# Routed experts: ten single-expert tiles and eight tiles of four 32-token units, copied matrices in homes of their own, rotary step ahead of the FFN norm

## What is computed

```python
x = x + layernorm(attention(layernorm(x)))   # 16 heads of 16; low-rank q and kv; rotary part added to q and k
x = x + layernorm(ffn(layernorm(x)))
# ffn, 2048 tokens, 8 experts, top 1:
logits = x @ router_w.T ; e = argmax ; score = sigmoid(top logit)
gate, up = split((x * score) @ gate_up_proj[e])   # 256 -> 2 x 512
routed   = (up * silu(gate)) @ down_proj[e]       # 512 -> 256
shared   = silu(x @ shared_gate_w) * (x @ shared_up_w) @ shared_down_w
```

## Time and profile before

| | us |
|---|---|
| median of three executions | 446.71 |
| lowest, highest | 446.14, 450.4 |
| the profiled execution, whole | 448.61 |
| its span (first to last instruction in the trace) | 446.8 |
| PE busy in it | 414.9 |
| DVE busy | 254.1 |
| ACT busy | 197.4 |
| POOL busy | 133.4 |

### The profile page before, as it was taken

One profiled execution on the slowest core, in us unless ns is written; L12 is line 12 of the kernel. 1 busy time (PEld: TensorE's weight loads), 2 busy tenths in 40 slices (PEclk: granted clock), 3 DMA queues, 4 the chain that ended last, 5 costly groups with the idle time before them and its releaser, 6 DMA issues.

```text
span 446.8 us, 8888 instructions
## 1 busy us (share of the span) xinstructions
PE 414.9 (93%) x3211; PEld 313.1 (70%) x3211; DVE 254.1 (57%) x601; ACT 197.4 (44%) x375; POOL 133.4 (30%) x186
## 2 busy tenths in 40 slices
PE   7998789999999999797989999999999999999990
PEld 6665456676676766374759999999997344489990
DVE  5474378787878777767655781322222334326685
ACT  1643747667676758456451123444444333211110
POOL 1334321616252524303302002222222010016872
PEclk9996999999999999899999999999999999999996
DMA  8699335355554536350157621111111111113432
GB/s 256 176 115 116 52 80 186 85 160 141 157 149 114 185 91 207 98 167 22 29 189 249 208 88 37 36 48 49 48 47 48 48 47 26 38 53 106 145 98 83
DMA packets 51137, 47.77 MB, mean 107 GB/s; under 512 B 5398, under 2 KB 45846, under 8 KB 51094
## 3 DMA queue, kind: packets, MB, share of 16 engines
q1 hardware_dynamic: 44779, 38.31, 32.9%
q0 software_dynamic: 1728, 4.72, 3.8%
q10 hardware_dynamic: 4587, 4.18, 2.7%
HBM read 25.44 MB, written 8.91 MB: 77 GB/s over the span
## 4 chain that ended last, share of the span: by engine, by line
PE 72%; DVE 10%; issue 5%; POOL 4%; DMA 3%; ACT 3%; SPq 1%; ACTq 0%; DVEq 0%; POOLq 0%
PE bank L1357 41%; PE bank L1676 6%; PE bank L1361 6%; PE bank L1545 4%; PE bank L1525 4%; PE bank L1693 3%; PE bank L1486 3%; DVE nmax L1028 2%; PE bank L1424 2%; POOL x_sb L656 1%; PE bank L1472 1%; DMA stacks<-mT 1%; SPq L517 1%; DVE wall L1058 1%; DVE stats_at L962 1%
## 5 line engine op out<-in xcount | busy, mean ns | idle before, releaser
L1028 DVE TENSOR_REDUCE nmax<-bank 128x2 f32<-128x512 f32 x112 | 74.2, 686 | 29.5 <-PE bank L1486 29.3
L1234 DVE TENSOR_TENSOR stacks<-stacks,bank 128x512 f32<-128x512 f32 x36 | 24.7, 687 | 69.0 <-PE bank L1357 61.4
L1357 PE MATMUL bank<-stacks,wall 128*128 128x128 f32 x512 | 61.2, 276 | 0.4 <-ACT stacks L890 0.4
L1357 PEld LDWEIGHTS bank<-stacks,wall 128*128 128x128 f32 x512 | 59.8, 192 | 2.5 <-issue 1.8
L854 ACT ACTIVATE pv<-bank 128x512 f32<-128x512 f32 x64 | 38.3, 606 | 36.4 <-PE bank L1545 35.6
L1545 PE MATMUL bank<-stacks 99*128 99x256 bf16 x256 | 49.5, 277 | 4.0 <-ACT wall L854 2.1
L1357 PE MATMUL bank<-wall,stacks 128*128 128x256 f32 (+1 forms) x224 | 53.0, 380 | 0.0
L687 POOL DMA_INDIRECT stacks<-x_sc,row_i x20 | 22.3, 1113 | 100.6 <-PE bank L1361 81.5
L890 ACT ACTIVATE stacks<-bank 128x512 f32<-128x512 f32 x36 | 21.5, 597 | 68.3 <-PE bank L1357 57.3
L854 ACT ACTIVATE wall<-bank 128x512 f32<-128x512 f32 x64 | 38.5, 606 | 28.6 <-PE bank L1545 27.5
L1486 PE MATMUL bank<-stacks 96*128 96x256 bf16 x224 | 42.5, 273 | 7.2 <-DVE nmax L1028 6.8
(11 more groups left out here) (198 smaller groups left out, 699.3 us busy)
## 6 DMA issues: line engine op xcount, KB each, us to landing
wall<-gate_up SPq DMA_DIRECT2D x8, 1024.0 KB, 5.3
stacks<-parts_k SPq DMA_DIRECT2D x72, 64.0 KB, 2.6
stacks<-parts_q SPq DMA_DIRECT2D x72, 64.0 KB, 2.5
wall<-down SPq DMA_DIRECT2D x8, 512.0 KB, 6.7
y_exp<-stacks ACTq DMA_DIRECT2D x20, 128.0 KB, 1.7
x_tok<-wall SPq DMA_DIRECT2D x8, 256.0 KB, 2.5
stacks<-x_tok SPq DMA_DIRECT2D x16, 128.0 KB
out<-stacks SPq DMA_DIRECT2D x8, 256.0 KB
```

Source lines behind the costliest of these rows:

```text
L1028: dve.tensor_reduce(nmax[:, half, qt, 2 * pair:2 * pair + 2], two(sm_bank[u % 2]), AX.X, ALU.max, negate=True).then_inc(sm["sm_max"], 1)
L1234: dve.tensor_tensor(to, sg, fu[:, :], ALU.mult).then_inc(sm["h_sb"], 1)
L1357: last = pe.matmul(out_ap, lhsT, rhs, start=(n == 0), stop=(n == len(pairs) - 1))
```

## The change

- Units are of 32 tokens (UT = 4 to a tile). FT falls from 12 to 10, NU rises from 16 to 32, NPT stays at 8, and NR falls from 20 to 18. POOL issues 18 gathers of tokens instead of 20.
- In a Q tile four matmuls of 32 columns stand side by side. Units 1 to 3 read copies: three gate, three up and three down matrices, nine copies of 128x1024 elements per tile where there were three. Each has one home: `extra_sb`, `wq_sb`, `wdo_sb` for gate, three quarters of `pv` for up, the fourth quarter and the two halves of the first 2048 columns of `low_sb` for down. To that end `wd_sb` and `wo_sb` become parts of one tensor, and so do `parts` and `wkv_sb`.
- A copy waits until its home has been read for the last time: gate copies for `g_ps`, up copies for `u_ps`, down copies for `y_ps` of the tile before. DVE makes six of the nine (one gate, two up, three down), ACT three (two gate, one up). PE waits for them by `gate_dve`, `gate_act`, `up_dve`, `up_act` and `down_dve`.
- In a Q tile that is followed two tiles later by another, `x_turn` moves from behind up to right behind `h_turn`, between gate and up.
- In the attention slots DVE runs `A_T` at head 1 ahead of `E_xn2`, which moves there from head 0.

The diff, cut to its core:

```diff
-U = P // 2
-FT = NT - E // 2
-NU = 2 * -(-(NT * 2 + E - 1 - 2 * FT) // 2)
-NPT = NU // 2
+UT = 4
+U = P // UT
+FT = NT - E * (P - U) // P
+NU = UT * -(-(NT * UT + E - 1 - UT * FT) // UT)
+NPT = NU // UT
...
-        wd_sb = sb("wd_sb", [P, KT, D])
+        wdo_sb = sb("wdo_sb", [P, 2, KT, D])
+        wd_sb, wo_sb = wdo_sb[:, 0, :, :], wdo_sb[:, 1, :, :]
         wq_sb = sb("wq_sb", [P, KT, 2 * D])
-        wkv_sb = sb("wkv_sb", [P, 3 * D])
+        low_sb = sb("low_sb", [P, 2 * NPART * S + 3 * D])
+        wkv_sb = low_sb[:, 2 * NPART * S:2 * NPART * S + 3 * D]
+        extra_sb = sb("extra_sb", [P, 2 * I])
         wrp_sb = sb("wrp_sb", [P, KT, P])
         rope_t = sb("rope_t", [P, S])
-        wo_sb = sb("wo_sb", [P, KT, D])
...
+        parts = {k: low_sb[:, NPART * S * n:NPART * S * (n + 1)].bitcast(BF16)
+                 .rearrange("p (a m c) -> p a m c", a=NPART, m=2) for n, k in enumerate("qk")}
...
-        d_tile = wq_sb[:, :, :].rearrange("p k c -> p (k c)")
+        unit_w = ((extra_sb[:, :], wq_sb[:, :, :].rearrange("p k c -> p (k c)"),
+                   wdo_sb[:, :, :, :].rearrange("p a k c -> p (a k c)")),
+                  tuple(pv[:, 2 * I * n:2 * I * n + 2 * I] for n in range(UT - 1)),
+                  (pv[:, 2 * I * (UT - 1):2 * I * UT], low_sb[:, 0:2 * I], low_sb[:, 2 * I:4 * I]))
+        unit_w = [[t.rearrange("p (k c) -> p k c", k=k) for t in ts] for ts, k in zip(unit_w, (KT, KT, I // P))]
...
+        def unit_weights(eng, seq, n, side):
+            eng.wait_ge(*((sm["g_ps"], seq), (sm["u_ps"], seq), (sm["y_ps"], seq))[side])
+            e = eng.value_load(eid_i[0:1, ds(unit_of(seq, n), 1)], min_val=0, max_val=E - 1)
+            flat = wall[:, :, :].rearrange("p e w -> p (e w)")
+            if side == 2:
+                of = flat[:, ds(e * WLEN + KT * 2 * I, D * I // P)].rearrange("p (k c) -> p k c", k=I // P)
+            else:
+                of = flat[:, ds(e * WLEN, KT * 2 * I)].rearrange("p (k c) -> p k c", k=KT)[:, :, I * side:I * side + I]
+            return unit_w[side][n - 1], of
...
-                        " L:8 L:9 L:10 L:11 L:12 L:13 L:14 L:15 L:16 L:17 L:18 L:19 L:20 L:21 L:22 L:23 L:24 L:25 L:26 L:27")
+                        " L:8 L:9 L:10 L:11 L:12 L:13 L:14 L:15 L:16 L:17 L:18 L:19 L:20 L:21 L:22 L:23 L:24 L:25")
...
+            def unit_copy(seq, n, side):
+                to, of = unit_weights(act, seq, n, side)
+                act.activation(to, of, ACT.Copy).then_inc(sm[("gate_act", "up_act")[side]], 1)
...
+                if kinds[2:] == "R":
+                    tile_second(seq + 2, p)
+                if kinds[2:] == "Q":
+                    unit_copy(seq + 2, 2, 0)
                 if kinds[2:] in ("R", "Q"):
-                    tile_second(seq + 2, p)
                     xT_copy(seq + 2, p)
+                if kinds[2:] == "Q":
+                    unit_copy(seq + 2, 3, 0)
+                    unit_copy(seq + 2, 3, 1)
...
-            order = {0: ("E_xn2",), 1: ("A_T",), 2: ("B_stats",), 3: ("B_norm",), 5: ("E_router",),
+            order = {1: ("A_T", "E_xn2"), 2: ("B_stats",), 3: ("B_norm",), 5: ("E_router",),
...
-            def tile_down(seq):
-                if seq == P0:
-                    dve.wait_ge(sm["inv_ps"], 1)
-                else:
-                    dve.wait_ge(sm["y_ps"], seq)
-                e = dve.value_load(eid_i[0:1, ds(unit_of(seq, 1), 1)], min_val=0, max_val=E - 1)
-                dve.tensor_copy(d_tile, wall[:, :, :].rearrange("p e w -> p (e w)")[:, ds(e * WLEN + KT * 2 * I, D * I // P)]
-                                ).then_inc(sm["w_down"], 1)
+            def unit_copy(seq, n, side):
+                to, of = unit_weights(dve, seq, n, side)
+                dve.tensor_copy(to, of).then_inc(sm[("gate_dve", "up_dve", "down_dve")[side]], 1)
...
-                    tile_down(seq)
+                if kinds[2:] == "Q":
+                    unit_copy(seq + 2, 1, 0)
                 if kinds[1:]:
                     hidden(seq + 1, 1 - p)
+                if kinds[2:] == "Q":
+                    unit_copy(seq + 2, 1, 1)
+                    unit_copy(seq + 2, 2, 1)
+                if kinds[1:2] == "Q":
+                    for n in range(1, UT):
+                        unit_copy(seq + 1, n, 2)
...
-                    for n, w in enumerate((flat_w[:, ds(e * WLEN + at, I)], w_tile[:, p, at:at + I])):
+                    for n, w in enumerate([flat_w[:, ds(e * WLEN + at, I)]] + [t[:, k, :] for t in unit_w[r]]):
...
+            def turns(kinds):
+                def f(seq, p):
+                    h_turn(seq, p)
+                    if kinds[2:] == "Q":
+                        x_turn(seq + 2, seq // 2 + 1, p)
+                return f
...
-                pe.wait_ge(sm["w_down"], seq - P0 + 1)
+                pe.wait_ge(sm["down_dve"], (UT - 1) * (seq - P0 + 1))
                 pe.wait_ge(sm["ys_sb"], seq - 1)
                 for k in range(I // P):
-                    for n, w in enumerate((flat_w[:, ds(e * WLEN + KT * 2 * I + D * k, D)], d_tile[:, D * k:D * k + D])):
+                    for n, w in enumerate([flat_w[:, ds(e * WLEN + KT * 2 * I + D * k, D)]] + [t[:, k, :] for t in unit_w[2]]):
...
+                        pe.wait_ge(sm[("gate_dve", "up_dve")[r]], (1 + r) * (seq - P0 + 1))
+                        pe.wait_ge(sm[("gate_act", "up_act")[r]], (2 - r) * (seq - P0 + 1))
...
-                    gate_and_up(seq + 1, 1 - p, then, h_turn if kind == "Q" else nothing)
-                if kinds[2:] in ("R", "Q"):
+                    gate_and_up(seq + 1, 1 - p, then, turns(kinds) if kind == "Q" else nothing)
+                if kinds[2:] in ("R", "Q") and kind != "Q":
```

More of the change, by code:

```diff
@@ L164, in program @@
         xn2T = spare2[:, 2560:3072].rearrange("p (k c) -> p k c", k=KT)
-        parts = {"q": sb("parts_q", [P, NPART, 2, S], BF16), "k": sb("parts_k", [P, NPART, 2, S], BF16)}
+        parts = {k: low_sb[:, NPART * S * n:NPART * S * (n + 1)].bitcast(BF16)
+                 .rearrange("p (a m c) -> p a m c", a=NPART, m=2) for n, k in enumerate("qk")}
         full = {"q": qf, "k": kf}
@@ L297, in program @@
             rt rt_exp lmax_ready oh_ready rank_ps tiles_ready ranked inv_in inv_ps rows_ready xr_in0 xr_in1 back_ready xr_ready xs_out0 xs_out1
-            xl_in0 xl_in1 xT_ps xT_sb g_ps u_ps sg_sb h_sb hT_ps hT_sb w_down w_first w_second y_ps ys_sb y_out0 y_out1
+            xl_in0 xl_in1 xT_ps xT_sb g_ps u_ps sg_sb h_sb hT_ps hT_sb w_first w_second gate_dve gate_act up_dve up_act down_dve y_ps ys_sb y_out0 y_out1
             gathered0 gathered1 gathered2 gathered3 gathered4 gathered5 gathered6 gathered7 z_ready zn_ready fin_ready fin_last out_done0 out_done1""".split()
@@ L426, in unit_of @@
         def unit_of(seq, n):
-            return FT + 2 * (seq - P0) + n
+            return FT + UT * (seq - P0) + n
+        def unit_weights(eng, seq, n, side):
[7 more added lines that the diff above has]
+            return unit_w[side][n - 1], of
         def tile_weights(eng, seq, p, k):
@@ L437, in tile_weights @@
                 eng.wait_ge(sm["u_ps"], seq - 1)
-            at = seq - R0 if seq < P0 else unit_of(seq, 1)
-            e = eng.value_load(eid_i[0:1, ds(at, 1)], min_val=0, max_val=E - 1)
+            e = eng.value_load(eid_i[0:1, ds(seq - R0, 1)], min_val=0, max_val=E - 1)
             return w_tile[:, p, 2 * I * k:2 * I * k + 2 * I], \
@@ L1716, in gate_and_up @@
                 if kind in ("R", "Q"):
+                    pe.wait_ge(sm["xT_sb"], seq - R0 + 1)
+                else:
+                    tokens_in(seq, p)
+                if kind == "R":
                     w = tile_w(p)
@@ L1719, in gate_and_up @@
                     pe.wait_ge(sm["w_second"], seq - R0 + 1)
-                    pe.wait_ge(sm["xT_sb"], seq - R0 + 1)
-                else:
-                    tokens_in(seq, p)
                 if kind == "Q":
```

## The result

The kernel after takes 431.09 us (median of 5 runs, 429.76 to 432.65), the kernel before 446.71 (5 runs, 446.14 to 450.78). The ratio is 0.9616, with an interval of 0.9575 to 0.9657. That is 17.1 us less by the ratio, 15.6 by the medians; predicted were 13.0. 0.9616 x 446.71 is 429.6 us, just under the low end of the range, 431.0. The direction was right and the size too small.

What follows compares the result with a forecast made beforehand. PE was taken as the bound, busy 414.9 of 446.8 us. Terms of -11.0 (tiles), -1.5 (x_turn), -0.8 (rotary order) and +0.3 (waits) gave -13.0, so 446.7 became 433.7 us, with a range from 431.0 to 438.0.

Steps and rivals of the forecast that it cites:

- Fewer tiles: R stage on PE: two R tiles of 5.52 us go and no Q tile comes, -11.0 us.
- Four units in a Q tile: Q tiles on PE: four units share the array as two do, difference 0, bounds 0 and 3.1 us.
- Rival C: Q tiles: four units don't share the array and go two by two, +43 us, 477; chance 0.02.
- x_turn moved: Q tiles on PE: 0.24 us saved in each of six bodies, 1.5 in all; a Q tile takes 6.18 us.
- Nine copies: Q tiles: DVE's eight instructions take 6.1 of 6.18 us, ACT's work 5.4; +0.2 us for added waits in all.
- Rival A: Q tiles: VectorE sets the pace, waits make it 6.6 us a tile, 436.6 us in all; chance 0.13.
- Rival B: DVE's copies in rows of 512 lose pace: 444.3 us if three (chance 0.05), 455.5 if six (0.03).
- The +0.1 at the change from R to Q: ACT's second gate copy is ready at about 5.5 us, PE wants it at 5.52: +0.1 us.
- The gather beside the copies: POOL's gather, issued almost two tiles ahead, may be late beside DVE's copies but doesn't reach PE: 0 us.
- Rotary ahead of the FFN norm: Attention slots 2 to 5: `A_T` ends earlier and PE's wait goes, -0.8 us, bounds -1.3 and +1.0.
- Rival D: Attention slots: the reordering makes PE wait for maxima instead, +1.0 in place of -0.8, 435.5 us; chance 0.08.
- Homes under other names, 12 more columns of constants and two gathers fewer cost nothing on PE: Allocation, constants and gathers: 0 us on PE.

Runs made afterwards that it cites:

- the experiment that removed them: Kernel after with ScalarE's gate copy of the fourth unit ahead of `xT_copy` in the last two R tiles: 432.28 us, ratio 0.9646 to before.
- homes alone: Kernel before with its tensors laid out as after the change (`low_sb`, `wdo_sb`, an unused `extra_sb`), nothing else: 448.72 us, ratio 1.0020.
- the second set: Kernel after measured once more, unchanged, beside the experiments: 432.06 us against 448.43 for before, ratio 0.9632.
- the shift alone: Kernel before with 12 unused columns more, in the constants (446.67 us, ratio 0.9959) or as a pad behind them (446.51 us, 0.9945).

## Why the prediction was right in direction and too small

The steps on tiles and copies held. What failed is the zero for the 12 columns of constants, and the term for the rotary order was little more than half of what it measured (0.8 against 1.4). The range didn't cover this: its low end of 431.0 is 2.7 under the forecast, but the bounds worked out on that side give 0.5 for the rotary order and 0.3 for the waits, and nothing for addresses or clock. The prediction's "up to -1.3 - 1.5" counts terms again that its sum already holds.

**Fewer tiles: right.** Predicted -11.0, measured -10.9 in the R stage. The R tiles stand 5.5 us apart.

**Four units in a Q tile: right.** I took 0 between bounds of 0 and 3.1. Four records start together at 0.43 us a step, two took 0.44. Rival C (477) is out: no group doubled.

**x_turn moved: right in sum, wrong as a step.** The tile is 6.11 us for a predicted 6.18. But the experiment that puts x_turn back shows the move to be worth 4.0 us in the Q stage and 4.3 to 4.6 in the time of this kernel, not 1.5: with four units and their copies on ACT, a late x_turn holds up the gate copy. I worked out what PE issues and not what ACT has queued behind its wait for it. Nothing of this fell into the sum, since the waits stood at 0 for the order as it is.

**Nine copies: right, with too narrow a margin.** PE doesn't wait for DVE. Rival A (436.6) didn't come about, and its price stood on 0.76 us per instruction, where seven copies on DVE point to 0.72 on the mean (an estimate). Rival B is out at its root: rows of 512 keep 0.69 us, as the Trainium skill has it (VectorE: DVE Perf Modes, Mode 2×_2P, the split on the outermost dimension). The +0.1 at the change from R to Q was two waits for ACT, shown as 0.25 us each; the experiment that removed them gained 0.3 us in all; for the other +0.2 PE's rows show no wait.

**The gather beside the copies: right.** Beside DVE's copies it takes up to 1.21 us, alone 0.94, and PE doesn't wait for it. The prediction set this against the rule of a lock for a whole instruction (the Trainium skill, SBUF — State Buffer, SBUF: two separate sides), as if 0.25 us were less than the rule asks. The ends of the records say that it isn't: the gather of the earlier trace rows ends at 328.39 + 1.19 = 329.58, 0.12 us behind the end of the copy that began within it (328.77 + 0.69), and so do 15 of the 16 gathers of before and 10 of the 11 of after within which such a copy began and ended. In the two others the copy began in the first 0.04 us of the gather, which still took 0.94. The reverse shows too: the copy at 339.48 outlasts the gather by 340.30 - 339.79 = 0.51 us and is 0.13 us longer than alone. This agrees with the rule, each waiting for the other's end. A gather held up by two or three copies, for which the prediction worked out a price, stands in no row.

**Rotary ahead of the FFN norm: the first term that was mis-sized.** Predicted -0.8, measured -1.3 to -1.9 at equal clock, -1.4 to -1.5 by the lengths of four slots. The step "PE's idle time for it is 0.9 us over the whole run" failed: idle time is counted from modelled ends and shows 0.33 of 0.41 us in the slot read, and 0.9 over a run in which four slots became 1.4 us shorter together. The distance between starts shows it whole. Rival D is out: PE's waits for maxima are 6.2 us in 12 places in after (6.8 in 13 before), and idle time at A_QK is 0.1 us over the run. The group in after:

```profile
L1455 PE MATMUL bank<-wall,wq_sb 64*128 64x256 f32 x32 | 9.0, 401 | 0.1
```

**"Homes under other names, 12 more columns of constants and two gathers fewer cost nothing on PE": the step that failed.** It holds for the names (homes alone: ratio 1.0020). The two gathers fewer were not tested by themselves. It doesn't hold for the columns: they are worth 0.7 to 1.0 us at equal clock through the addresses behind them, and 1.7 to 1.9 by the mean times, with the clock that went with them. The step that put them at nothing gave no reason. A sign or size for this could not be read from the trace of before; what I could have given is a bound on both sides in place of a bare zero.

**What wasn't in the sum: the level of the clock.** The mean granted clock is 0.9752 over the runs of before and 0.9820 over those of after (0.9797 in the second set). At 0.29 us per 0.001 that is 1.3 to 2.0 us. About 0.9 of it went with the shift alone; for the rest no edit is shown.

The sum as measured, at equal clock: R tiles -10.9, Q tiles -1.7, order -1.4, addresses -0.7 to -1.0, together -14.7 to -15.0 for a measured -15.1 and -14.8 in the two sets of after. With the clock it is -16.7 to -17.0 for the -17.1 of the first set and -16.0 to -16.3 for the -16.1 of the second (mean times). At equal clock the parts add up within the noise; 0.4 to 1.1 us of clock stay without a cause.

## What to carry to other kernels

Where PE is the bound in all stages, tiles removed and tiles packed came through in full here, and their price could be read from the spacing of starts. Read a wait from the starts on both of its sides, not from the idle column, and when a step moves on one engine, look at what is queued behind its consumer on the next engine. A change of size in an allocation moves every address behind it. Here 48 bytes were worth 0.4 to 0.5% and 10,240 bytes nothing, so leave a term of about half a per cent on both sides, and test it with a pad that nothing uses. Look at the granted clock of a stage before you read a gain from it: one kernel needed 74.49 and 77.27 us for the same stage, at 0.98 and 0.93.

## What the runs showed of the hardware that was not expected

- 48 bytes more in front of the tensors made the wait for a transfer within SBUF 0.91 to 0.99 us where it was 1.34 to 1.38: eight profiled executions against three, with no overlap. The mean granted clock was higher too. The cause is open.
- DVE's instructions last 0.68 to 0.69 us each but can start 0.60 apart (338.88 to 339.48); in other places they start 0.76 to 0.83 apart. What decides it is not shown.
- A gather of POOL within which a copy of DVE starts and ends lasts until 0.12 us behind the copy's end, 1.05 to 1.21 us in place of 0.94 (25 of 27 in before and after). A copy that begins in the last 0.2 to 0.4 us of a gather takes 0.72 to 0.88 us in place of 0.69, and ends 0.51 us behind it.
- Between runs of one kernel, stretches of about 5 us at a lower clock come and go. Windows in before and in after that have one; the kernel with the gate copy first has 1.00 in both:

```profile
185.00:190.00 5.00, 4.53 (x31) 2.05 (x32) 2.47 (x5) 2.04 (x4) 0.66 (x2) 0.66 0.40 104
```

```profile
175.00:180.00 5.00, 3.91 (x29) 1.68 (x28) 3.85 (x11) 1.76 (x4) 2.65 (x6) 0.66 0.39 97
```
